# The bank shared by a graph network's second product and its last block of sums: zeroed each group, or overwritten and its sums carried away

## The chip, the core and the metric

The kernel runs on one core of a Trainium2 chip. The metric is the time of one execution on the device in microseconds (us), the median of several runs. TensorE multiplies matrices into PSUM (8 banks of 512 f32 columns by 128 partitions); VectorE, ScalarE and GpSimd work element by element, and the latter also issues the indirect transfers (gathers); SyncE (SP) and ScalarE issue plain ones.

## The reference, cut to what matters

Four graph layers in a row work on 3125 nodes with 16 features and 103125 edges sorted by one end. The second, called L1, is the one that the change touches. It has four layers itself, with 128 hidden features:

```python
h = h @ emb_w + emb_b
for i in range(4):
    ef = concat([h[row], h[col], edge_attr])
    ef = silu(ef @ edge_w1[i] + edge_b1[i])
    ef = silu(ef @ edge_w2[i] + edge_b2[i]) * edge_mask
    agg = segment_sum(ef, row, num_segments=n)
    nf = silu(concat([h, agg]) @ node_w1[i] + node_b1[i])
    h = (h + nf @ node_w2[i] + node_b2[i]) * node_mask
```

## The kernel before

Nodes are padded to 25 blocks of 128 (NB = 25, NP = 3200); the last block has 53 real nodes (3125 - 3072). Edges are in tiles of 128, and three tiles (M3) make a group: 280 groups (G3) in each of the four layers, in turns of U3 = 8, 35 turns (K3). Turns 0, 1 and 34 are written out; the others are a hardware loop, so each engine has a branch after every eight groups.

update(layer) writes two tables to memory: p_tab and q_tab, h times the two halves of the first edge weight. edge_mlp(layer) then does for each group, with one semaphore per kind of work:

- SP and ScalarE load the p_tab blocks (pb) for the group; SP loads also q_tab blocks (qb), and rows for the one-hot matrices. GpSimd gathers rows of q_tab by index (L1613), two tiles of a group, and three in every fourth group (nine gathers in four groups). VectorE writes the indices (L1764) five groups ahead.
- VectorE builds the one-hot matrices ohn and oht (L1784, L1785) one group ahead, and ohm (L1793, three per group).
- TensorE's first(): all parts of the first product are added into z1, 384 columns of bank 7 (L1655, L1658, L1660, and the gathers by a transposing matmul, L1663). It waits for the gathers ahead of L1663, and raises m_z1.
- ScalarE's one(): silu from z1 into h1 (L1729), raises m_h1.
- TensorE's second(): three matmuls of h1 with w2 into z2 (L1673), raises m_z2.
- VectorE's add(): z2 + b2 into h2 (L1771), raises m_add; then it waits for that add, and sets z2 to zero (L1774), raising m_zero.
- ScalarE's two(): silu of h2 in place (L1734), raises m_h2.
- TensorE's sums(): three matmuls of h2 with ohm (L1683), each added onto the columns of the block that the tile's edges belong to; the address is a register. It raises m_sum.

PSUM is full: the sums of all 25 blocks fill columns 0 to 3199 for the whole of a layer, z1 is columns 3584 to 3967 and z2 3200 to 3583. So bank 6 (columns 3072 to 3583) holds both the last block's sums and z2. Matmuls with start=False add onto what stands there; a start=True in that bank would touch the bookkeeping of the whole bank. That is why z2 is set to zero by VectorE and the second product is added onto the zeros.

The order on each queue, for group n, is:

- TensorE: first(n), sums(n-3), second(n-1). sums(n-3) waits for zero(n-2), second(n-1) for the same.
- VectorE: add(n-2) with its memset, build(n+1), indices(n+5), build_m(n-2).
- ScalarE: two(n-2), one(n), and issues of loads between.

After the groups, update(layer) copies the sums out of PSUM (bank 6 by VectorE, L1960) and goes on with the node part. Each line below carries the number that the profile uses.

Of the kernel before, what the change touches and what calls it, by code (L numbers as in the profile page):

```python
# [54 lines left out]
def gnn_kernel(nc, a, out):  # L55

    with ExitStack() as ctx:
# [1441 lines left out]
        with ExitStack() as st:  # L1499
# [63 lines left out]
        m_idx, m_oht, m_ohm, m_z1, m_h1, m_z2, m_add, m_zero, m_h2, m_sum = (  # L1563
            sem("m_" + n) for n in ("idx", "oht", "ohm", "z1", "h1", "z2", "add", "zero", "h2", "sum"))
        m_got = [sem(f"m_got{h}") for h in range(U3)]
        m_pl, m_sp, m_act = ([sem(f"m_{n}{q}") for q in range(U3 // 2)] for n in ("pl", "sp", "act"))
        Z1, Z2 = 3584, NP

        def edge_mlp(layer, we36, w2, b1, b2):
# [18 lines left out]
            with ExitStack() as st:  # L1588
# [11 lines left out]
                z1, z2 = ps[:, Z1:Z1 + GW], ps[:, Z2:Z2 + GW]  # L1600

                with nc.Block() as block:
# [38 lines left out]
                    def _(pe):  # L1641
# [23 lines left out]

                        def second(k, h):

                            n = k * U3 + h
                            if layer or here(k, h, 1):
                                pe.wait_ge(m_zero, g0 + n)  # L1670
                            pe.wait_ge(m_h1, g0 + n + 1)
                            for j in range(M3):
                                m = pe.matmul(z2[:, j * P:(j + 1) * P], h1[:, h % 2, j * P:(j + 1) * P], w2, start=False, stop=True, skip_group_check=True)  # L1673
                            m.then_inc(m_z2, 1)

                        def sums(k, h, after=2):
# [3 lines left out]
                            pe.wait_ge(m_zero, g0 + n + after)  # L1680
# [10 lines left out]
                        def step(k, h):  # L1691
                            if h % 2 == 0 and here(k, h, 2):
                                take(*moved(k, h, -2))
                            first(k, h)
                            if here(k, h, 3):
                                sums(*moved(k, h, -3))
                            if here(k, h, 1):
                                second(*moved(k, h, -1))
                        turns(pe, step, K3, U3)
                        take(K3 - 1, U3 - 2)  # L1700
                        sums(K3 - 1, U3 - 3)
                        second(K3 - 1, U3 - 1)
                        sums(K3 - 1, U3 - 2)
                        take(K3 - 1, U3 - 1)
                        sums(K3 - 1, U3 - 1, 1)
# [51 lines left out]
                    def _(dve):  # L1757
# [8 lines left out]
                        def add(k, h):  # L1766
                            n = k * U3 + h
                            if here(k, h, 2):
                                dve.wait_ge(m_sum, g0 + n - 1)
                            dve.wait_ge(m_z2, g0 + n + 1)  # L1770
                            dve.tensor_tensor(h2[:, h % 2, :, :], z2.rearrange("p (j f) -> p j f", j=M3),  # L1771
                                              b2[:, None, :].to_broadcast([P, M3, HID]), ALU.add).then_inc(m_add, 1)
                            dve.wait_ge(m_add, g0 + n + 1)
                            dve.memset(z2, 0.0).then_inc(m_zero, 1)  # L1774
# [29 lines left out]

                        for h in range(5):
                            indices(0, h)
# [5 lines left out]
                        build_m(K3 - 1, U3 - 1)  # L1812

        with ExitStack() as st:
# [14 lines left out]
            b2 = sb("b2", [P, L, HID], F32, st)  # L1829
            xT = sb("xT1", [FIN, NP], F32, st)  # L1830
# [347 lines left out]
```

## Time and profile before

| | us |
|---|---|
| median of 3 runs | 8277.64 |
| lowest and highest | 8270.27, 8279.68 |
| the profiled execution | 8273.71 |
| its span | 8272.0 |
| TensorE busy, whole span | 6199.3 |
| TensorE weight loads busy | 5285.4 |
| GpSimd busy | 5228.1 |
| VectorE busy | 5187.0 |
| ScalarE busy | 2895.5 |

The span is the time from the first to the last instruction in the profile; the execution's own time has 1.7 us around it. Busy times are sums over the whole span, in which four functions of very different character follow each other, so their shares have to be read by stretch. In a row of grouped instructions, out<-in are the program's names, x is the count, then come the busy us, the mean ns of one, and the idle us of that engine just before them with what ended that idle time; "issue" means that nothing that the profile shows ended it. One matmul of f32 operands counts as two records.

### The profile page before, as it was taken

Reading aid. Unit: us, or ns where it says so; the run is one execution under the profiler, and the core shown is the slowest. Engines: PE = TensorE matmul, PEld = TensorE weight load, DVE = VectorE, ACT = ScalarE, POOL = GpSimd, SP = SyncE. Lnnn points to the kernel's source line nnn. Section 1 sums busy time; section 2 is a strip of 40 time slices with the busy share of each in tenths; the row PEclk is TensorE's granted clock in tenths of the full one; section 3 lists DMA queues with packets and bytes.
Section 4 is the critical chain, followed back from the end, with each engine's and each line's share of the span. In section 5 each row is a group of like instructions: output and inputs, shape, how many; then the busy total and the mean of one; then the engine's idle time right before and its main releaser. Section 6 shows DMA issues by size and latency. Waiting matters only on the chain. (4 is left out here: it accounts for less than half of the span.)

```text
span 8272.0 us, 234007 instructions
## 1 busy us (share of the span) xinstructions
PE 6199.3 (75%) x55084; PEld 5285.4 (64%) x55143; DVE 5187.0 (63%) x14678; ACT 2895.5 (35%) x8539; POOL 5228.1 (63%) x7407
## 2 busy tenths in 40 slices
PE   2222215767789998999899989999976667888998
PEld 1111113555478886888688868887575556887998
DVE  6333346867567775777577757776432225998998
ACT  3222202545433333333333333333233332222554
POOL 3777754756477776777677767776677774222554
PEclk7555556555599999999999999999555556999999
DMA  5000013434378786878688768886300001332332
GB/s 162 5 3 3 3 38 107 120 96 120 88 221 220 220 220 176 222 222 222 179 222 222 222 174 227 222 222 183 101 6 7 7 7 38 82 82 56 73 72 59
DMA packets 1322718, 1020.15 MB, mean 123 GB/s; under 512 B 479756, under 2 KB 1223586, under 8 KB 1321696
## 3 DMA queue, kind: packets, MB, share of 16 engines
q1 hardware_dynamic: 938010, 667.14, 29.2%
q0 software_dynamic: 134272, 178.98, 9.2%
q10 hardware_dynamic: 250308, 172.51, 7.2%
q8 instruction: 57, 0.93, 0.0%
q14 instruction: 71, 0.58, 0.0%
HBM read 951.88 MB, written 73.77 MB: 124 GB/s over the span
## 5 line engine op out<-in xcount | busy, mean ns | idle before, releaser
L1613 POOL DMA_INDIRECT qg<-q_tab,qidx x2520 | 2421.6, 961 | 873.1 <-issue 610.1
L1163 PE MATMUL ps<-rhs_i,ohi 128*128 128x128 f32 (+2 forms) x8640 | 1215.2, 266 | 209.8 <-issue 197.7
L1734 ACT ACTIVATE h<-h 128x384 f32<-128x384 f32 x1120 | 585.8, 523 | 1910.4 <-DVE h L1771 1824.0
L1163 PEld LDWEIGHTS ps<-rhs_i,ohi 128*128 128x128 f32 (+1 forms) x8640 | 998.6, 162 | 342.2 <-issue 281.2
L1683 PE MATMUL ps<-ohm,h 128*128 128x128 f32 x6720 | 1029.8, 289 | 226.0 <-issue 213.2
L1129 POOL COPY near<-x 128x48 bf16 x2160 | 676.0, 351 | 774.3 <-PE ps L1152 432.2
L1771 DVE TENSOR_TENSOR h<-ps,b 128x384 f32<-128x384 f32 x1120 | 623.9, 557 | 823.2 <-PE ps L1673 779.0
L1683 PEld LDWEIGHTS ps<-ohm,h 128*128 128x128 f32 x6720 | 834.5, 191 | 456.5 <-issue 456.3
L1314 POOL DMA_INDIRECT got_m<-y_tab,idx_m x832 | 831.1, 999 | 330.3 <-issue 248.7
L407 POOL DMA_INDIRECT list_by_src<-ring,rpos x808 | 783.1, 969 | 333.2 <-issue 253.9
L1793 DVE TENSOR_SCALAR ohm<-iota_row,loc_p,w_p 128x128 f32<-128x128 f32 x3360 | 966.0, 350 | 0.1
L1673 PE MATMUL ps<-w,h 128*128 128x128 f32 x6720 | 936.5, 276 | 0.0
L1224 DVE TENSOR_TENSOR ohi<-iota_row,dst_i 128x512 f32<-128x512 f32 (+1 forms) x1080 | 927.9, 859 | 0.0
L1338 PE MATMUL ps<-rhs_m,ohi_m 128*128 x2880 | 662.0, 403 | 321.3 <-ACT rhs_m L1370 290.4
L1338 PEld LDWEIGHTS ps<-rhs_m,ohi_m 128*128 128x128 f32 x2880 | 634.6, 328 | 350.2 <-issue 350.1
L1673 PEld LDWEIGHTS ps<-w,h 128*128 128x128 f32 x6720 | 843.3, 193 | 0.5 <-DVE ps L1774 0.2
L1658 PE MATMUL ps<-oht,pb 128*128 128x128 bf16 x10080 | 750.1, 220 | 0.0
L1729 ACT ACTIVATE h<-ps,b 128x384 f32<-128x384 f32 x1120 | 649.9, 580 | 209.0 <-PE ps L1663 116.1
L1658 PEld LDWEIGHTS ps<-oht,pb 128*128 128x128 bf16 x10080 | 661.1, 98 | 82.6 <-issue 1.9
L1400 DVE TENSOR_TENSOR ohi_m<-iota_row,dst_i 128x512 f32<-128x512 f32 x360 | 249.1, 693 | 727.4 <-PE ps L1338 727.4
L1219 DVE TENSOR_SCALAR oht_i<-places_i,iota_p 128x512 bf16<-128x512 bf16 (+1 forms) x1080 | 510.4, 473 | 192.9 <-PE ps L1163 161.4
L1127 POOL COPY near<-z 128x384 bf16 x720 | 345.4, 509 | 365.4 <-PE ps L1152 303.5
(448 smaller groups left out, 8921.1 us busy)
## 6 DMA issues: line engine op xcount, KB each, us to landing
pb<-p_tab ACTq DMA_DIRECT2D x1680, 96.0 KB
pb<-p_tab SPq DMA_DIRECT2D x1680, 96.0 KB
places<-place_by_turn SPq DMA_DIRECT2D x560, 192.0 KB
places_i<-place_by_meeting SPq DMA_DIRECT2D x360, 256.0 KB, 3.4
places_i<-place_by_meeting SPq DMA_DIRECT2D x720, 128.0 KB, 3.1
qb<-q_tab SPq DMA_DIRECT2D x840, 64.0 KB
qg<-q_tab,qidx POOLq DMA_INDIRECT x2520
nears<-near_by_turn SPq DMA_DIRECT2D x560, 64.0 KB
```

Of the source, the lines that this page charges most:

```text
L407: pool.indirect_dma_start(list_s[:, :], IndirectOffsetOnAxis(ap=rpos[:, h, c:c + 1], axis=0), ring[:, h, c, :], None).then_inc(scattered[h ...
L1129: m = pool.tensor_copy(near[:, h, j, :], table[:, bass.ds(at[j], 48)])
L1163: m = pe.matmul(ps[:, bass.ds(to[j], width)], ohi[:, h, j, :], rhs[:, h, j, 0:width], start=False, stop=True, skip_group_check=True)
L1224: dve.tensor_tensor(ohi[:, h, :, :], iota_row[:, None, :].to_broadcast([P, M, P]), dst_i[:, bass.ds(n * M, M)][:, :, None].to_broadcast([P ...
L1314: pool.indirect_dma_start(got[:, h, j, :], None, y_tab, IndirectOffsetOnAxis(ap=idx[:, h, j:j + 1], axis=0)).then_inc(d_got[h], 16)
L1338: m = pe.matmul(ps[:, bass.ds(to[j], 32)], ohi[:, h, j, :], rhs[:, bass.ds(at[j], 1), :].rearrange("p t f -> p (t f)"), start=False, stop= ...
L1613: pool.indirect_dma_start(qg[:, h, j, :], None, q_tab, IndirectOffsetOnAxis(ap=qidx[:, h, j:j + 1], axis=0)).then_inc(m_got[h], 16)
L1658: pe.matmul(z1[:, j * P:(j + 1) * P], pb[:, h, j, q_ * HID:(q_ + 1) * HID], oht[:, h, j * P:(j + 1) * P], start=False, stop=False)
L1673: m = pe.matmul(z2[:, j * P:(j + 1) * P], h1[:, h % 2, j * P:(j + 1) * P], w2, start=False, stop=True, skip_group_check=True)
L1683: m = pe.matmul(ps[:, bass.ds(to[M3 * (1 - h % 2) + j], P)], h2[:, h % 2, j, :], ohm[:, h % 2, j, :], start=False, stop=True, skip_group_c ...
L1729: act.activation(h1[:, h % 2, :], z1, ACT.Silu, bias=b1).then_inc(m_h1, 1)
L1793: m = dve.tensor_scalar(ohm[:, h % 2, j, :], iota_row[:, :], loc_p[:, bass.ds(t, 1)], w_p[:, bass.ds(t, 1)], ALU.is_equal, ALU.mult)
```

## The change

- The second product is written with start=True, so z2 needn't be zero: the memset and m_zero go.
- After the three matmuls of second(), fresh() writes zeros with start=True to `part`, the 53 real columns of the last block's sums in bank 6 (a bf16 matmul of a zero tile). m_z2 is raised by it. The sums that follow add onto these zeros.
- So what the last block has gathered must leave the bank each group: add() has a second tensor_tensor, `rim += part`, with rim a tile [128, 53] in SBUF, and it is that one that raises m_add.
- TensorE's order becomes first(n), second(n-1), sums(n-3). second(n-1) waits for m_add of group n-2. The sums wait for ohm and h2 alone.
- add(n-2) waits for m_sum of group n-4, and by the order on TensorE that covers m_z2 of n-2.
- rim is zeroed at the start of a layer, and at its end VectorE adds the last part; update() copies rim in place of bank 6's columns. The columns of aggT behind N are zeroed once.

```diff
--- before.py
+++ after.py
@@ -1560,13 +1560,13 @@
                         root_step(act, b_to + 2)
 
 
-        m_idx, m_oht, m_ohm, m_z1, m_h1, m_z2, m_add, m_zero, m_h2, m_sum = (
-            sem("m_" + n) for n in ("idx", "oht", "ohm", "z1", "h1", "z2", "add", "zero", "h2", "sum"))
+        m_idx, m_oht, m_ohm, m_z1, m_h1, m_z2, m_add, m_h2, m_sum = (
+            sem("m_" + n) for n in ("idx", "oht", "ohm", "z1", "h1", "z2", "add", "h2", "sum"))
         m_got = [sem(f"m_got{h}") for h in range(U3)]
         m_pl, m_sp, m_act = ([sem(f"m_{n}{q}") for q in range(U3 // 2)] for n in ("pl", "sp", "act"))
-        Z1, Z2 = 3584, NP
-
-        def edge_mlp(layer, we36, w2, b1, b2):
+        Z1, Z2, FEW = 3584, NP, N - (NB - 1) * P
+
+        def edge_mlp(layer, we36, w2, b1, b2, rim):
 
 
             g0, k0 = layer * G3, layer * K3
@@ -1598,6 +1598,7 @@
                 h1 = sb(f"h1{layer}", [P, 2, GW], F32, st)
                 h2 = sb(f"h2{layer}", [P, 2, M3, HID], F32, st)
                 z1, z2 = ps[:, Z1:Z1 + GW], ps[:, Z2:Z2 + GW]
+                part = ps[:, NP - P:NP - P + FEW]
 
                 with nc.Block() as block:
                     @block.gpsimd
@@ -1663,21 +1664,24 @@
                                 m = pe.matmul(z1[:, j * P:(j + 1) * P], qg[:, h, j, :], ident[:, :], start=False, stop=(j == gathered(h) - 1), is_transpose=True)
                             m.then_inc(m_z1, 1)
 
+                        def fresh():
+
+                            return pe.matmul(part, nothing[:, 0:P], nothing[:, 0:FEW], start=True, stop=True)
+
                         def second(k, h):
 
                             n = k * U3 + h
                             if layer or here(k, h, 1):
-                                pe.wait_ge(m_zero, g0 + n)
+                                pe.wait_ge(m_add, g0 + n)
                             pe.wait_ge(m_h1, g0 + n + 1)
                             for j in range(M3):
-                                m = pe.matmul(z2[:, j * P:(j + 1) * P], h1[:, h % 2, j * P:(j + 1) * P], w2, start=False, stop=True, skip_group_check=True)
-                            m.then_inc(m_z2, 1)
-
-                        def sums(k, h, after=2):
+                                pe.matmul(z2[:, j * P:(j + 1) * P], h1[:, h % 2, j * P:(j + 1) * P], w2, start=True, stop=True)
+                            fresh().then_inc(m_z2, 1)
+
+                        def sums(k, h):
 
                             n = k * U3 + h
                             pe.wait_ge(m_ohm, g0 + n + 1)
-                            pe.wait_ge(m_zero, g0 + n + after)
                             pe.wait_ge(m_h2, g0 + n + 1)
                             for j in range(M3):
                                 m = pe.matmul(ps[:, bass.ds(to[M3 * (1 - h % 2) + j], P)], h2[:, h % 2, j, :], ohm[:, h % 2, j, :],
@@ -1692,17 +1696,19 @@
                             if h % 2 == 0 and here(k, h, 2):
                                 take(*moved(k, h, -2))
                             first(k, h)
+                            if here(k, h, 1):
+                                second(*moved(k, h, -1))
                             if here(k, h, 3):
                                 sums(*moved(k, h, -3))
-                            if here(k, h, 1):
-                                second(*moved(k, h, -1))
                         turns(pe, step, K3, U3)
                         take(K3 - 1, U3 - 2)
+                        second(K3 - 1, U3 - 1)
                         sums(K3 - 1, U3 - 3)
-                        second(K3 - 1, U3 - 1)
+                        pe.wait_ge(m_add, g0 + G3)
+                        fresh()
                         sums(K3 - 1, U3 - 2)
                         take(K3 - 1, U3 - 1)
-                        sums(K3 - 1, U3 - 1, 1)
+                        sums(K3 - 1, U3 - 1)
 
                     @block.scalar
                     def _(act):
@@ -1767,11 +1773,13 @@
                             n = k * U3 + h
                             if here(k, h, 2):
                                 dve.wait_ge(m_sum, g0 + n - 1)
-                            dve.wait_ge(m_z2, g0 + n + 1)
+                            else:
+                                dve.wait_ge(m_z2, g0 + n + 1)
                             dve.tensor_tensor(h2[:, h % 2, :, :], z2.rearrange("p (j f) -> p j f", j=M3),
-                                              b2[:, None, :].to_broadcast([P, M3, HID]), ALU.add).then_inc(m_add, 1)
-                            dve.wait_ge(m_add, g0 + n + 1)
-                            dve.memset(z2, 0.0).then_inc(m_zero, 1)
+                                              b2[:, None, :].to_broadcast([P, M3, HID]), ALU.add)
+                            if layer or here(k, h, 1):
+                                dve.wait_ge(m_add, g0 + n)
+                            dve.tensor_tensor(rim, rim, part, ALU.add).then_inc(m_add, 1)
 
                         def build(k, h):
                             n, q = k * U3 + h, h // 2
@@ -1802,6 +1810,7 @@
                             if here(k, h, 2):
                                 build_m(*moved(k, h, -2))
 
+                        v_chain(dve, dve.memset(rim, 0.0))
                         for h in range(5):
                             indices(0, h)
                         build(0, 0)
@@ -1810,6 +1819,8 @@
                         build_m(K3 - 1, U3 - 2)
                         add(K3 - 1, U3 - 1)
                         build_m(K3 - 1, U3 - 1)
+                        dve.wait_ge(m_sum, g0 + G3)
+                        v_chain(dve, dve.tensor_tensor(rim, rim, part, ALU.add))
 
         with ExitStack() as st:
             hT = sb("hidT", [P, NP], F32, st)
@@ -1827,6 +1838,7 @@
             third = sb("third", [36, 3], BF16, st)
             part36 = sb("part36", [36, 2], F32, st)
             b2 = sb("b2", [P, L, HID], F32, st)
+            rim = sb("rim", [P, N - (NB - 1) * P], F32, st)
             xT = sb("xT1", [FIN, NP], F32, st)
             pq_out = [sem(f"pq_out{i}") for i in range(4)]
             pq_n = [0] * 4
@@ -1835,6 +1847,7 @@
                 @block.vector
                 def _(dve):
                     v_chain(dve, dve.memset(maskT[:, N:NP], 0.0))
+                    v_chain(dve, dve.memset(aggT[:, N:NP], 0.0))
                     v_chain(dve, dve.memset(eat[:, :, :], 0.0))
                     v_chain(dve, dve.memset(we36[:, :], 0.0))
                     for q, (lo, hi) in enumerate(((0, 12), (12, 24), (24, 36))):
@@ -1956,8 +1969,8 @@
                     def _(dve):
                         if not first:
                             for i in (0, 2, 4, 6):
-                                n = min(512, NP - 512 * i)
-                                dve.tensor_copy(aggT[:, 512 * i:512 * i + n], banks[i][:, 0:n]).then_inc(u_sum_v.sem, 1)
+                                n = min(512, N - 512 * i)
+                                dve.tensor_copy(aggT[:, 512 * i:512 * i + n], rim[:, :] if i == 6 else banks[i][:, 0:n]).then_inc(u_sum_v.sem, 1)
 
                         if first:
                             dve.wait_ge(mask_in, 32)
@@ -2018,7 +2031,7 @@
 
             update(-1)
             for layer in range(L):
-                edge_mlp(layer, we36[:, layer * HID:(layer + 1) * HID], w2[:, layer, :], b1[:, layer:layer + 1], b2[:, layer, :])
+                edge_mlp(layer, we36[:, layer * HID:(layer + 1) * HID], w2[:, layer, :], b1[:, layer:layer + 1], b2[:, layer, :], rim[:, :])
                 update(layer)
             nodes([(hT, wout[:, :])], FIN, 0)
             b_to, b_fr = to_act.base(1), from_act.base(1)
```

## Rows read from the trace of the kernel before

**Rows 1.** The page's costliest groups: busy us, mean ns, then idle us before and releasers.

```profile
L1613 POOL DMA_INDIRECT qg<-q_tab,qidx x2520 | 2421.6, 961 | 873.1 <-issue 610.1
...
L1314 POOL DMA_INDIRECT got_m<-y_tab,idx_m x832 | 831.1, 999 | 330.3 <-issue 248.7
```

**Rows 2.** Busy time by stretch, one of L1's four steady ones: us, engines, clock, DMA.

```profile
3185.00:4010.00 825.00, 758.79 (x7186) 674.37 (x7186) 575.07 (x2154) 308.22 (x559) 601.59 (x625) 1.00 0.79 219
```

**Rows 3.** Groups of instructions by line, 3200 to 3900 us, same columns.

```profile
L1683 PE MATMUL ps<-ohm,h 128*128 128x128 f32 x1434 | 219.6, 289 | 44.1 <-issue 41.2
```

**Rows 4.** Timeline of one group: start us, us, engine, line.

```profile
3272.35 0.56 DVE L1771 TENSOR_TENSOR h<-ps,b 128x384 f32<-128x384 f32 x1 [0.70 <-PE ps L1673]
...
3272.94 0.52 ACT L1734 ACTIVATE h<-h 128x384 f32<-128x384 f32 x1 [1.75 <-DVE h L1771]
...
3273.06 0.38 DVE L1774 MEMSET ps<- 128x384 f32 x1 [0.15 <-DVE h L1771]
...
3273.09 0.38 PE L1663 MATMUL ps<-ident,qg 128*128 128x128 f32 x2
3273.35 0.22 DVE L1784 TENSOR_SCALAR ohn<-nears,iota_p 128x128 f32<-128x128 bf16 x1
3273.47 0.26 DVE L1785 TENSOR_SCALAR oht<-places,iota_p 128x384 bf16<-128x384 bf16 x1
3273.53 0.58 ACT L1729 ACTIVATE h<-ps,b 128x384 f32<-128x384 f32 x1
...
3273.64 0.93 PE L1683 MATMUL ps<-ohm,h 128*128 128x128 f32 x6 [0.17 <-issue]
...
3274.41 0.83 PE L1673 MATMUL ps<-w,h 128*128 128x128 f32 x6
...
3275.07 0.33 PE L1655 MATMUL ps<-eat,we 128*128 128x384 bf16 x1
...
3275.28 0.56 DVE L1771 TENSOR_TENSOR h<-ps,b 128x384 f32<-128x384 f32 x1 [0.68 <-PE ps L1673]
```

**Rows 5.** Timeline of TensorE where the loop branch falls.

```profile
3280.26 0.83 PE L1673 MATMUL ps<-w,h 128*128 128x128 f32 x6
3281.43 0.33 PE L1655 MATMUL ps<-eat,we 128*128 128x384 bf16 x1 [0.33 <-issue]
3281.60 0.67 PE L1658 MATMUL ps<-oht,pb 128*128 128x128 bf16 x9
3282.10 0.44 PE L1660 MATMUL ps<-ohn,qb 128*128 128x128 f32 x2
...
3283.93 0.33 PE L1655 MATMUL ps<-eat,we 128*128 128x384 bf16 x1
```

**Rows 6.** Timeline of GpSimd, the gathers.

```profile
3289.40 0.94 POOL L1613 DMA_INDIRECT qg<-q_tab,qidx  x1 [0.80 <-DVE qidx L1764]
...
3324.41 0.94 POOL L1613 DMA_INDIRECT qg<-q_tab,qidx  x1 [1.71 <-DVE qidx L1764]
...
5757.05 0.94 POOL L1613 DMA_INDIRECT qg<-q_tab,qidx  x1 [0.30 <-issue]
```

**Rows 7.** Groups of instructions by line, whole span.

```profile
L1976 DVE TENSOR_TENSOR left<-ps,p_out 128x128 f32<-128x128 f32 x100 | 28.3, 289 | 72.9 <-ACT q_out L1946 72.4
```

**Rows 8.** Waits of SP's queue, 3200 to 3900 us: us, times, longest.

```profile
SPq L1626 <- PE ps L1663: 97.3, 111, 1.5
```

**Rows 9.** Timeline of TensorE, last sums of the fourth layer.

```profile
5775.29 0.93 PE L1683 MATMUL ps<-ohm,h 128*128 128x128 f32 x6 [0.18 <-issue]
```

**Rows 10.** Timeline of the second layer's beginning.

```profile
3178.94 0.97 POOL L1613 DMA_INDIRECT qg<-q_tab,qidx  x1 [3.50 <-DVE qidx L1764]
...
3186.51 0.50 PE L1655 MATMUL ps<-eat,we 128*128 128x384 bf16 x1 [5.41 <-DMA pb<-p_tab]
```

**Rows 11.** Timeline of the third function, GpSimd and ScalarE.

```profile
6302.05 0.94 POOL L1314 DMA_INDIRECT got_m<-y_tab,idx_m  x1 [0.30 <-issue]
...
6304.56 0.85 ACT L1365 ACTIVATE gate_m<-got_m,hea_s 128x1 f32<-128x1 f32 x4 [3.15 <-DMA got_m<-y_tab,idx_m]
```

## The prediction

> **What bounds the kernel now.** I read the page's costliest groups first [rows 1]: GpSimd's gathers (L1613) lead them. The second layer function, L1, runs from about 2288 to 5776 us, four layers of 280 groups (1120 calls of each line), and there no engine is full. So I cut it into the four steady stretches [rows 2]: in each of 825 us TensorE is busy 759, GpSimd 602, VectorE 575, ScalarE 308, at a granted clock of 1.00 and a DMA share of 0.79. TensorE at 92% has about 66 us of holes per layer. The grouped rows of 700 us [rows 3] say where: 44 us ahead of the sums' matmuls (L1683), under "issue", that is, on a semaphore that the profile does not name.
>
> The timeline of one group names it [rows 4]. The add (L1771) starts at 3272.35, the memset of the second product's columns ends at 3273.06 + 0.38 = 3273.44, and the sums start at 3273.64. The transposed gathers (L1663) had begun at 3273.09; a run of such matmuls gives way to the next about 0.16 before its recorded end (L1673 lasts 0.83, L1655 begins 0.66 later), so the sums could have begun at 3273.31. TensorE waits 0.33 us for m_zero. The loop that sets the pace is: add 0.56, own semaphore 0.15, memset 0.38, to TensorE 0.20, sums 0.77, second product 0.66, and 0.21 from the next group's first matmul (3275.07) to the next add (3275.28). That is 2.93, and 2.92 to 2.93 is the spacing of L1655. What TensorE needs by itself is seen where the loop branch has put it late, so that the memset is no longer waited for [rows 5]: 3281.43 to 3283.93, 2.50 us. The branch itself costs TensorE 1.17 - 0.67 = 0.50 us in eight groups (3280.26 to 3281.43).
>
> Behind TensorE stands GpSimd, and close. Its gathers of 0.94 follow each other with holes of 0.30 us [rows 6], and the holes are 0.30 too where VectorE's indices are called the releaser. So 0.30 is GpSimd's own. Over all of L1 there are 2520 gathers of 0.961 us with 873.1 us of holes [rows 1]. Two kinds of longer hole exist. One of 0.80 (3289.40) stands once or so in a turn of eight groups and ahead of a group's first gather: that is a wait for the indices, which VectorE writes five groups ahead. The other is 1.7 to 1.95 us long and stands ahead of the second gather of a group, where the code waits for nothing; it comes every 99 gathers, at the same places in every layer, 6 times per layer (the one at 3324.41 in rows 6). I take it as GpSimd's own.
>
> **GpSimd's floor.** 4 x 630 gathers x (0.961 + 0.305) = 3190.3 us, and 24 holes x about 1.54 above 0.305 = 37.0, together 3227 us; per group 3227 / 1120 = 2.88. What it takes now is 2421.6 + 873.1 less the four holes ahead of a layer's first gather (about 3.5 each, 14.1; one in rows 10) = 3280.6. The difference, 54 us, is all that its waits for TensorE's pace are worth.
>
> **The change, part by part.** *The memset goes* (1120 x 0.378) and with it VectorE's wait for its own add (0.15). *The add into rim comes*: tensor_tensor of 128x53 f32 from PSUM. The trace has 128x384 at 0.56 us (L1771) and 128x128 at 0.289 (L1976) [rows 4, 7], a slope of 1.06 ns a column, so 53 columns are about 0.21 us. At most it is L1976's 0.29; how little it is doesn't matter, since TensorE's own time, below, is then the longer. It waits only for the rim add before it, long done, and VectorE's instructions without a wait between them overlap a little (L1784 of 0.22 at 3273.35, L1785 at 3273.47 [rows 4]), so I let it end 0.69 after the add starts; if it can't overlap, 0.77. *fresh()* is one bf16 matmul of 53 columns and its weight load: nine L1658 take 0.50 us (3281.60 to 3282.10) [rows 5], so 0.06; nothing at the least, since a weight load can go ahead; at worst weight load 0.10 and matmul 0.33, unhidden like a lone L1655, 0.42. *The order* first, second, sums moves the wait of VectorE's add from m_z2 to m_sum, but both are the end of TensorE's step; and the wait for VectorE moves from the sums to the second product, at the same place behind first(). The sums lose their m_zero wait and wait for ohm and h2 of three groups back, both done a step earlier.
>
> The new loop: 0.69, to TensorE 0.20, second 0.66, fresh 0.06, sums 0.77, 0.21 = 2.59. TensorE's own: 2.50 + 0.06 + 0.50/8 = 2.62. So TensorE and VectorE want 2.62 to 2.67 per group where GpSimd wants 2.88: **GpSimd becomes the bound**, and the change is worth what it lets GpSimd give.
>
> The Trainium skill, "VectorE: DVE Perf Modes", section "The DRAIN you can't avoid", says that the next VectorE operation does not start until the pipe is empty. By that the rim add ends at 0.77, the loop is 2.67 and the sum below stays; here L1785 starts 0.10 before L1784 ends, so the trace does not quite agree.
>
> What else is queued: m_add now comes from the rim add, so ScalarE's second silu (L1734) starts about 0.13 later than now (3272.94), ends 1.24 after the add, and L1729, which now starts 1.18 after it (3273.53), slips by 0.06; its result is wanted by the next L1655 at 2.4. Covered by sums and second product; without that cover it would cost its 0.06. VectorE's queue behind the adds (ohn, oht, indices, ohm) moves earlier by about 0.4. SP's queue waits for TensorE 97.3 us in 700 (111 times) [rows 8], so it has room for 2.88.
>
> **Edges of a layer, x4.** Now GpSimd is done well ahead: last gather ends 5757.05 + 0.94 = 5757.99, sums end 5775.29 + 0.93 = 5776.22, 18.2 later [rows 6, 9]. Bound by GpSimd, that lead is used up (it begins as 3186.51 - 3178.94 = 7.6 us [rows 10], and 0.2 per group eats it within some 40 groups). After the last gather: landing 1.6 (in the third function ScalarE starts 1.57 after a gather's end [rows 11]; bounds 0.3 and 2.8), transposes 0.34, second 0.72, sums 0.77 = 3.43; 0.21 + 0.69 + 0.20 + 0.72 + 0.77 = 2.59 for group 279's second product and the sums of 277; 0.21 + 0.69 + 0.20 + 0.06 + 0.77 + 0.93 for the rest = 2.86: 8.9, and the last rim add with its semaphores 0.36: 9.2. Gain 9.0. The memset of rim ahead of the indices delays the first gather by about 0.25 (a small operation and 0.15). Net 8.7 per layer, 35 in all. The other edits (aggT's pad once, 53 columns instead of 128 in one copy) are under 0.5 us.
>
> **Sum.** 54 + 35 = 89 us. The profiled execution took 8273.7 (span 8272.0 and 1.7 around it), so 8185; against the median of 8277.6, **8188 us**.
>
> **Rivals.** A change of 0.2% (16.6 us) is about what a measurement can tell from none.
> 1. *GpSimd binds* (8188, own range 8165 to 8215, from the landing, 0.30 or 0.31 for a hole, and the 24 long holes): 0.68.
> 2. *The VectorE-TensorE loop still binds.* With every price at its upper end, 0.56 + 0.15 + 0.29 + 0.20 + 0.66 + 0.15 + 0.77 + 0.21 = 2.99, nothing is won; from 2.88 up it decides. For it: every group now waits there. Against: a wait and 0.17 of length are plainly gone. At 2.90 for the present mean of 2.935 (825 us, less edges, for 280 groups) it gives 39 us, and no lead is used: 8238. 0.10.
> 3. *Gathers grow.* They are the bound, and L1314's take 999 ns where these take 961 [rows 1]. 38 ns x 2520 = 96 us eats the 89: 8285, no change. Against: until a layer's first long hole, 87 gathers run free in 3289.4 - 0.5 - 3178.94 = 110.0 us [rows 6, 10], 1.264 each, the same price. 0.08.
> 4. *Gathers shrink.* Most take 0.94 [rows 6] and the mean is 0.961, so at most 21 ns x 2520 = 53 us: 8135. 0.08. The Trainium skill, "DMA: Bandwidth & Descriptors", section "SWDGE vs HWDGE vs iDMA", says that GpSimd writes its descriptor rings in SBUF and that VectorE can lock it out in its two-port modes. By that rule a denser VectorE would lengthen gathers and a removed memset would shorten them; no row here separates the two.
> 5. *Slower: fresh() is not pipelined.* A bf16 weight load and matmul wedged between f32 runs, on TensorE, each group, at 0.42 us: 2.56 + 0.42 = 2.98 against 2.935, x 1120 = +50 us: 8328. It decides from 0.375 us. For it: such a pair stands alone nowhere in the trace. Against: L1655 follows f32 matmuls 0.66 behind, as they follow each other. 0.06.
>
> **Numbers.** Faster: 0.68 + 0.08 + 0.07 of rival 2 = 0.83. Same: rival 3 and a little of 2, 0.09. Slower: 0.08, rival 5 and the upper tails of 2 and 3. The range of 8140 to 8265 takes in 1, nearly all of 4 and the faster part of 2, and leaves out some 0.19.
>
> **What the profile of the changed kernel would show.** GpSimd's holes ahead of L1613 all 0.30 but for the 24 long ones, "DVE qidx" as releaser nearly gone; TensorE waiting for gathers ahead of the transposes in first(), and no wait ahead of sums or second product; spacing of groups 2.88 with two-gather groups shorter and three-gather groups longer; last gather to last sums about 9 us; rim adds of 0.21. I am wrong if the wait reappears ahead of the second product (rival 2), if L1613's mean moves from 961, or if the pair of fresh() takes over 0.3 us.

## The result, and the profile after

Before, in the runs beside it: 8274.6 us (8270.3 to 8279.7, four runs). After: **8127.3 us** (8124.0 to 8131.0, four runs). The ratio is 0.9822, with a 95% interval of 0.9805 to 0.9839: 147 us, 1.8%. The forecast was 8188 with a range of 8140 to 8265. It had the direction and the new bound, and a gain of 89 us where 147 came; the time lies below the range. One later execution, of the changed kernel with TensorE's old order, took 10256 us at a mean granted clock of 0.54, where the others had 0.79; it is left out below and not explained.

The profiled execution took 8131.0 (span 8129.3, against 8272.0: 142.7 less). The page's costliest groups (busy, mean ns of one, idle before and its releasers) show GpSimd's gathers, the sums' matmuls and the transposes:

```profile
L1614 POOL DMA_INDIRECT qg<-q_tab,qidx x2520 | 2398.8, 952 | 781.9 <-issue 647.9
...
L1687 PE MATMUL ps<-ohm,h 128*128 128x128 f32 x6720 | 1024.6, 289 | 0.7 <-issue 0.7
...
L1664 PE MATMUL ps<-ident,qg 128*128 128x128 f32 x2520 | 479.6, 281 | 158.4 <-DMA qg<-q_tab,qidx 154.9
```

The wait ahead of the sums (L1687) is gone: 0.7 us in all of L1, where it was 44.1 in 700 us alone [rows 3]. TensorE now waits for gathered rows ahead of the transposes. GpSimd's idle time fell by 91.2 and its busy time by 22.8 [rows 1]. A layer fits in less than 825 us, so the busy time of each engine is read over 780 us of the second layer (columns as in [rows 2]):

```profile
3150.00:3930.00 780.00, 735.53 (x7428) 691.77 (x7428) 535.84 (x2147) 306.68 (x557) 589.05 (x619) 1.00 0.83 229
```

GpSimd is busy 589 and idle 191 there, at 1.26 us a gather, and TensorE is still at 94%. The groups by line of 3200 to 3900 us:

```profile
L1614 POOL DMA_INDIRECT qg<-q_tab,qidx x557 | 529.9, 951 | 169.9 <-issue 146.1 <-DVE qidx L1770 22.6 <-PE ps L1664 1.2
...
L1782 DVE TENSOR_TENSOR rim<-rim,ps 128x53 f32<-128x53 f32 x248 | 49.7, 200 | 0.0
L1669 PE MATMUL ps<-nothing 128*128 128x53 bf16 x248 | 46.6, 188 | 0.0
```

169.9 us of idle time ahead of 557 gathers is 0.305 each, whoever is called the releaser, so that is the floor. The longest single waits of GpSimd in that stretch, by the waits view, are 0.3 too:

```profile
POOL qg L1614 <- issue: 146.1, 479, 0.3
POOL qg L1614 <- DVE qidx L1770: 22.6, 74, 0.3
```

Where the kernel before has one of its long holes, behind the 113th gather of the layer (1.71 us [rows 6]), the timeline of GpSimd has nothing; the last line is the same gather:

```profile
3275.84 0.94 POOL L1614 DMA_INDIRECT qg<-q_tab,qidx  x1 [0.30 <-issue]
3277.08 0.94 POOL L1614 DMA_INDIRECT qg<-q_tab,qidx  x1 [0.30 <-issue]
3278.33 0.99 POOL L1614 DMA_INDIRECT qg<-q_tab,qidx  x1 [0.30 <-issue]
```

The timeline of TensorE (start, length, then any wait) has two groups without a wait, 2.61 apart, and one of three gathers that waits:

```profile
3324.82 0.33 PE L1656 MATMUL ps<-eat,we 128*128 128x384 bf16 x1
...
3325.98 0.83 PE L1678 MATMUL ps<-w,h 128*128 128x128 f32 x6
3326.65 0.19 PE L1669 MATMUL ps<-nothing 128*128 128x53 bf16 x1
3326.68 0.91 PE L1687 MATMUL ps<-ohm,h 128*128 128x128 f32 x6
3327.43 0.33 PE L1656 MATMUL ps<-eat,we 128*128 128x384 bf16 x1
...
3330.04 0.33 PE L1656 MATMUL ps<-eat,we 128*128 128x384 bf16 x1
3330.20 0.67 PE L1659 MATMUL ps<-oht,pb 128*128 128x128 bf16 x9
3331.29 0.55 PE L1664 MATMUL ps<-ident,qg 128*128 128x128 f32 x3 [0.42 <-DMA qg<-q_tab,qidx]
...
3333.12 0.33 PE L1656 MATMUL ps<-eat,we 128*128 128x384 bf16 x1
```

VectorE's two adds and ScalarE's two silu of the first of these groups, from the timeline of all engines:

```profile
3325.02 0.56 DVE L1778 TENSOR_TENSOR h<-ps,b 128x384 f32<-128x384 f32 x1 [0.81 <-PE ps L1687]
3325.49 0.20 DVE L1782 TENSOR_TENSOR rim<-rim,ps 128x53 f32<-128x53 f32 x1
3325.73 0.52 ACT L1740 ACTIVATE h<-h 128x384 f32<-128x384 f32 x1 [1.58 <-DVE rim L1782]
...
3326.32 0.58 ACT L1735 ACTIVATE h<-ps,b 128x384 f32<-128x384 f32 x1
```

TensorE's timeline at the end of the fourth layer, behind the last gather (5620.92 + 0.94 = 5621.86):

```profile
5623.42 0.55 PE L1664 MATMUL ps<-ident,qg 128*128 128x128 f32 x3 [0.38 <-DMA qg<-q_tab,qidx]
...
5626.18 0.94 PE L1678 MATMUL ps<-w,h 128*128 128x128 f32 x6 [0.77 <-DVE rim L1782]
...
5629.95 0.96 PE L1687 MATMUL ps<-ohm,h 128*128 128x128 f32 x6 [0.17 <-issue]
5632.45 1.12 PE L1908 MATMUL ps<-hidT,wn 128*128 128x512 f32 x2 [1.54 <-DVE aggT L1973]
```

**Where the 142.7 us came from.** From the first gather's start to the last one's end the four layers took 825.7, 818.1, 818.7 and 818.2 us before, and 791.2, 791.3, 791.5 and 791.8 after: 114.7 less. Each gather's own hole, sorted by its length in the two timelines, splits it. Short holes above the floor of 0.305 gave 54.6 (there are none after). The 24 long ones gave 37.0 (none after). The gathers themselves gave 22.8. These make 114.4 of it. Of the 142.7, the other 28.0 lie outside the gathers, at the layers' edges.

### The profile page after: what moved, and what is told of

Same layout as the page of the kernel before. It is cut to its first block and busy times, and to the rows that moved or that the text cites. A ratio compares the mean times of both kernels' runs of the same rounds, so it can differ in the third digit from the quotient of the medians.

```text
span 8129.3 us, 235796 instructions
## 1 busy us (share of the span) xinstructions
PE 6145.4 (76%) x56208; PEld 5382.7 (66%) x56267; DVE 5038.0 (62%) x14687; ACT 2897.6 (36%) x8539; POOL 5208.7 (64%) x7407
## 5 line engine op out<-in xcount | busy, mean ns | idle before, releaser
L1687 PE MATMUL ps<-ohm,h 128*128 128x128 f32 x6720 | 1024.6, 289 | 0.7 <-issue 0.7
L407 POOL DMA_INDIRECT list_by_src<-ring,rpos x808 | 784.2, 971 | 333.0 <-issue 254.2
L1687 PEld LDWEIGHTS ps<-ohm,h 128*128 128x128 f32 x6720 | 839.0, 192 | 14.7 <-issue 1.4
L1664 PE MATMUL ps<-ident,qg 128*128 128x128 f32 x2520 | 479.6, 281 | 158.4 <-DMA qg<-q_tab,qidx 154.9
```

What stands on the lines that cost most here:

```text
L407: pool.indirect_dma_start(list_s[:, :], IndirectOffsetOnAxis(ap=rpos[:, h, c:c + 1], axis=0), ring[:, h, c, :], None).then_inc(scattered[h ...
L1687: m = pe.matmul(ps[:, bass.ds(to[M3 * (1 - h % 2) + j], P)], h2[:, h % 2, j, :], ohm[:, h % 2, j, :], start=False, stop=True, skip_group_c ...
```

## The experiments

What each is for: the 37.0 us of long holes were forecast to stay, so they are the question. Either VectorE's memset, which the change removes, brought them out, or they come when GpSimd is held back, by whatever. The other questions are the price of fresh(), the order, and what lengthened the gathers.

The chips were not alike. On chips 13 and 1 the kernel before takes 8274 and 8279 us; on chips 14, 6 and 10 it takes 10259, 10393 and 10411. Each time and ratio below is against the kernel before on the same chip.

**The memset put back** (chip 13), behind the add of the changed kernel, with its semaphore:

```diff
-                    b2[:, None, :].to_broadcast([P, M3, HID]), ALU.add)
+                    b2[:, None, :].to_broadcast([P, M3, HID]), ALU.add).then_inc(m_zero, 1)
+                            dve.wait_ge(m_zero, g0 + n + 1)
+                            dve.memset(z2, 0.0)
```

> The changed kernel with the memset of z2 put back between VectorE's add and the rim add, with the wait for the add's own semaphore ahead of it; nothing is left out of the result. My theory: the loop of VectorE and TensorE is again longer than GpSimd's time. From the group spacing of 2.61 that the changed kernel shows when nothing waits for a gather, plus 0.15 + 0.38 = 3.14 us against 2.83 now: 8127 + 0.31 x 1120 + about 30 for the edges = 8500 us (8440 to 8540). Rival, that the memset was hidden all along and the gain came from the order: under 8200. On the 24 holes of 1.7 to 1.95 us ahead of second gathers: they should be back by both explanations that I hold open, that the memset causes them and that holding GpSimd back causes them; if they stay away, both are wrong.

Measured: 8363.5 us, ratio 1.0108 (1.0091 to 1.0125). That is 1.1% slower than before, but 137 us less than the 8500 expected, and outside the expected range. VectorE's timeline:

```profile
3403.92 0.56 DVE L1778 TENSOR_TENSOR h<-ps,b 128x384 f32<-128x384 f32 x1 [0.58 <-PE ps L1687]
3404.63 0.38 DVE L1781 MEMSET ps<- 128x384 f32 x1 [0.15 <-DVE h L1778]
3404.92 0.20 DVE L1784 TENSOR_TENSOR rim<-rim,ps 128x53 f32<-128x53 f32 x1
...
3406.92 0.56 DVE L1778 TENSOR_TENSOR h<-ps,b 128x384 f32<-128x384 f32 x1 [0.59 <-PE ps L1687]
```

The loop is 3.00, not 3.14. The rim add starts 0.09 before the memset's recorded end, and the next second product of TensorE (3405.17) follows the rim add's end at 0.05, where [rows 4] had led me to 0.20. The loop binds again, and the long holes are back: 6 per layer, 39.5 us in all, at gathers of a mean of 948 ns. So this run says that a bound loop brings the holes, but not whether the memset does.

**fresh() six times** (chip 13):

```diff
+                            for _ in range(5):
+                                fresh()
                             fresh().then_inc(m_z2, 1)
```

> The changed kernel with fresh() issued six times in place of once; nothing is left out of the result. This slows TensorE by 5 x 0.06 = 0.28 to 0.30 us a group and puts no memset anywhere: about 2.90 + 0.06 for the branch = 2.96 us a group, so that GpSimd is held back again: 8127 + 0.13 x 1120 + up to 30 for the edges = 8290 us (8230 to 8320). If the long holes come from GpSimd being held back, 24 of them are there again and gathers have a mean near 0.961. If they come from VectorE's memset, there are none, and the mean is near 0.950. If a fresh() costs far more than 0.06 the time shows it: at 0.19 each, the recorded length, 8127 + 0.78 x 1120 + 30 = 9030 us.

Measured: 8130.9, ratio 0.9825 (0.9809 to 0.9842), the time of the changed kernel. TensorE's timeline shows why:

```profile
3400.51 0.32 PE L1669 MATMUL ps<-nothing 128*128 128x53 bf16 x6
3400.66 0.91 PE L1689 MATMUL ps<-ohm,h 128*128 128x128 f32 x6
```

Six take 0.15 us from start to the sums' start, 0.026 each. TensorE wants 2.74 per group then (2.80 with the branch), still under 2.83, and nothing is held back: no hole over 0.32 in any layer. TensorE is busy 762.7 of the 780 us where the changed kernel has 735.5, and the layers take 789 to 791: 27 us more of TensorE's busy time cost nothing. My expectation had gone by the prediction's price of 0.06 for each, more than twice what was measured.

**The order of before** (chip 13): first product, sums, second product, the rest as in the changed kernel, with fresh() now ahead of the sums.

```diff
-                            fresh().then_inc(m_z2, 1)
+                            m.then_inc(m_z2, 1)
...
+                            if clear:
+                                pe.wait_ge(m_add, g0 + n + 2)
+                                fresh()
...
-                            if here(k, h, 1):
-                                second(*moved(k, h, -1))
                             if here(k, h, 3):
                                 sums(*moved(k, h, -3))
+                            if here(k, h, 1):
+                                second(*moved(k, h, -1))
```

> The changed kernel with TensorE's old order first, sums, second: fresh() stands ahead of the sums, which wait for the rim add, and VectorE's add waits for m_z2 again; nothing is left out of the result. Theory: the wait for VectorE stands behind first() either way, the loop stays at about 2.6 us and GpSimd binds at 2.83, so the time is 8127 within 16, with the holes of GpSimd all at 0.30. Rival, that the order carries part of the gain: waits ahead of the sums and 8160 or more.

Measured: 8122.9, 8123.0 and 8131.1, ratio 0.9823 (0.9804 to 0.9843). The layers take 790 to 792, without a hole over 0.32. The order is worth nothing here. Since the run with the memset put back lost the whole gain, what matters is that the memset and its wait left the loop.

**On chip 14**, four kernels: twelve fresh() (11 more in place of the 5 above), a memset that no one waits for, and both kernels with two gathers in every group.

```diff
+                            dve.memset(aside, 0.0)
```

stands between the add and the rim add, on columns of a tile in SBUF that is idle there (a tile of its own behind the rim add, off the loop, has no room left in SBUF, so that form was not measured), and

```diff
-                return 3 if h % 4 == 3 else 2
+                return 2
```

leaves out the third gather of every fourth group, so that those blocks' rows are not what the reference wants.

> The changed kernel with fresh() issued twelve times; nothing is left out of the result. Six of them left the time alone and took 0.155 us together, 0.026 each, so twelve add about 0.29 us a group: TensorE needs 2.61 + 0.29 + 0.06 for the branch = 2.96 against GpSimd's 2.83, and GpSimd is held back with no memset anywhere. Time: 8127 + 0.13 x 1120 + 15 to 30 for the edges = 8295 us (8250 to 8320). If the long holes ahead of second gathers come from holding GpSimd back, there are 24 again; if they come from VectorE's memset, there are none.

> The changed kernel with one more memset of 128x384 f32 per group on VectorE, into columns of a tile in SBUF that nothing uses meanwhile, between its two adds; nothing is left out of the result. VectorE's side of the loop has 0.24 us or more to spare against TensorE's 2.61 and more against GpSimd's 2.83, so GpSimd should still bind. If a memset disturbs GpSimd by itself (gathers that start just behind it take up to 1.19 in the kernel before), the gathers' mean rises from 0.951 to 0.960 or more and the time to 8150 to 8200 us, and long holes return if they are its work. If it was only the place of the memset in the loop that cost time: mean 0.95, no long hole, 8127 within 8.

> The changed kernel with two gathers in every group; it leaves out the third gather of every fourth group, and so a part of the first product of that tile. GpSimd then needs 2 x 1.257 = 2.51 us a group, less than TensorE's 2.60 on average (three groups of 2.61, one of 2.34, and 0.06 for the branch), so this shows what the loop alone costs after the change: 8127 - 0.22 x 1120 = 7880 us (7850 to 7930), and no wait ahead of the transposes. If something else than GpSimd stands behind the 2.83 (loads, ScalarE), less is won than 100 us.

> The kernel before with two gathers in every group; it leaves out the same part. There the loop over memset and semaphores sets the pace at 2.93, so GpSimd's shorter time should change nothing: 8274 within 12. With e7 it gives the change's worth where GpSimd doesn't bind, about 390 us or 0.33 a group. Long holes: if they come with GpSimd being held back they are there, at other places; if they belong to places in the order of gathers, every 99th still.

Measured, against 10258.8: 10642.3, ratio 1.0391 (1.0358 to 1.0423); 10349.1, 1.0101 (1.0072 to 1.0130); 9924.3, 0.9684 (0.9657 to 0.9712); 9797.6, 0.9556 (0.9524 to 0.9587). All four miss what was expected of them, and none tests what it was made for: L1 moves 140 to 164 GB/s there, against 219 in [rows 2]. Between the two kernels with two gathers the changed one is the slower by 1.3% (9924.3 against 9797.6). The first three come again on chip 1, and the last one on chips 6 and 10, below.

**Twelve fresh() again** (chip 1): no memset anywhere, but TensorE's step longer than GpSimd's floor. It is the run that tells the two theories of the long holes apart.

> The changed kernel with fresh() issued twelve times, again, since the last measurement was on a chip whose transfers are slower (the kernel before took 10259 us there). Same expectation: TensorE needs about 2.61 + 0.29 + 0.06 = 2.96 us a group against GpSimd's 2.83, GpSimd is held back with no memset anywhere, 8295 us (8250 to 8320). If the long holes ahead of second gathers come from holding GpSimd back, there are 24 again; if from VectorE's memset, none.

Measured: 8252.5, ratio 0.9970 (0.9957 to 0.9982), just at the lower edge of the expected range. GpSimd's timeline:

```profile
3559.42 0.94 POOL L1614 DMA_INDIRECT qg<-q_tab,qidx  x1 [0.30 <-issue]
3560.67 0.94 POOL L1614 DMA_INDIRECT qg<-q_tab,qidx  x1 [0.30 <-issue]
3563.55 0.94 POOL L1614 DMA_INDIRECT qg<-q_tab,qidx  x1 [1.94 <-PE ps L1664]
```

Six long holes in every layer again, 9.3 to 9.8 us of excess a layer, and 14 to 19 us of short ones. No memset runs in L1's groups. So the holes need no memset. Against six fresh() only TensorE's own time is longer, and the 24 holes are the difference: in L1 they come with a GpSimd that is held back.

**The memset aside again** (chip 1):

> The changed kernel with one more memset of 128x384 f32 per group into an idle SBUF tile between VectorE's two adds, again, on a chip with transfers as in the first measurements. If a memset disturbs GpSimd by itself: mean gather 0.960 or more and 8150 to 8200 us, with long holes if they are its work. If it was only its place in the loop that cost time: mean 0.95, no long hole, 8127 within 8.

Measured: 8197.2, ratio 0.9905 (0.9888 to 0.9921). VectorE's timeline shows that the memset did not stay aside:

```profile
3561.62 0.56 DVE L1778 TENSOR_TENSOR h<-ps,b 128x384 f32<-128x384 f32 x1 [0.35 <-PE ps L1687]
3562.21 0.38 DVE L1782 MEMSET nT<- 128x384 f32 x1
3562.50 0.15 DVE L1783 TENSOR_TENSOR rim<-rim,ps 128x53 f32<-128x53 f32 x1
...
3564.46 0.56 DVE L1778 TENSOR_TENSOR h<-ps,b 128x384 f32<-128x384 f32 x1 [0.54 <-issue]
```

The rim add starts 0.88 after the add, where it started 0.47 after it, and the loop is 2.84. I had reckoned 0.24 us of slack, and it was used up. The loop again just holds GpSimd: 21 long holes, layers of 802 to 804, gathers of 952 ns as after. A memset in every group did not lengthen the gathers. In the first layer GpSimd runs with holes under 0.33 up to its 204th gather, and the place behind the 113th passes without a hole; the five behind it have theirs. The third layer fits less well: its hole behind the 113th is 1.92, with nothing over 0.33 ahead of it.

**Two gathers in every group** of the changed kernel (chip 1), so that GpSimd's floor drops to 2 x 1.26 = 2.5 us per group:

> The changed kernel with two gathers in every group (it leaves out the third gather of every fourth group), again. GpSimd needs 2.51 us a group, TensorE about 2.60: 7880 us (7850 to 7930) and no wait ahead of the transposes. If something else than GpSimd stands behind the 2.83, less than 100 us is won.

Measured: 7933.6, ratio 0.9584 (0.9568 to 0.9600), just above the expected range. The window of 600 us in the second layer:

```profile
3200.00:3800.00 600.00, 590.92 (x6029) 559.41 (x6029) 437.62 (x1760) 250.84 (x454) 433.45 (x455) 1.00 0.88 242
```

TensorE is busy 98%, and the 600 us hold 228 groups, 2.63 each. The third gather thus costs the changed kernel 202 us. Here too GpSimd is held back, and here too there are long holes: five in every layer, behind the 113th gather and every 100th from there, and one of 1.32 behind the 60th in the second layer. They keep nearly to the count of gathers, though one group in four has a gather fewer.

**The changed kernel again** (chip 1):

> The changed kernel itself beside the other three, as it is. 8127 within 8 where the kernel before takes 8274. If this chip has the slower transfers (the kernel before at 10200 or more), the loads bind in both and the change is worth little or nothing: 10259 within 100, since TensorE then waits for loads in either order.

Measured: 8135.4, ratio 0.9826 (0.9810 to 0.9843), layers of 792 to 793, no hole over 0.32; that is 0.4 us over the expected 8127 within 8, where the kernel before takes 4 us more too. The gain and the absence of holes repeat on a second chip.

**Before with two gathers** (chips 6 and 10), and the changed kernel beside it on chip 10, to learn what the change does to the loop alone:

> The kernel before with two gathers in every group (it leaves out the third gather of every fourth group), again, on a chip with transfers as in the first measurements. The loop over the memset sets the pace at 2.93, so GpSimd's shorter time changes nothing: 8278 within 12. With e11 (7934) it gives the change's worth where GpSimd doesn't bind: about 345 us, against 147 where it does. Rival: if the 2.93 were partly GpSimd's, 8200 or less.

> The kernel before with two gathers in every group (it leaves out the third gather of every fourth group), once more. On a chip where the kernel before takes 8274 to 8279: 8278 within 12, since the loop over the memset sets the pace; with e11 (7934) the change is worth about 345 us where GpSimd doesn't bind. Rival: 8200 or less, if the 2.93 were partly GpSimd's. On a chip with slow transfers: about 9800 to 9920, as measured twice.

> The changed kernel itself. Where the kernel before takes 8274 to 8279: 8130 within 8. On a chip with slow transfers (the kernel before above 10200): TensorE waits for loads in both, and in the variants with two gathers the new one was the slower there (9924 against 9798), so between 10250 and 10450, no gain or a loss of up to 1.5%.

Measured: 9922.1 against 10393.3, ratio 0.9543 (0.9505 to 0.9582); 9941.9 against 10411.1, 0.9554 (0.9538 to 0.9570), both just above the 9920 expected at most for such a chip; and the changed kernel 10519.4, **1.0099** (1.0080 to 1.0118), which is slower than before and outside what was expected (10250 to 10450). Both chips were again of the slower kind, so the loop alone was not measured at full transfer speed. The changed kernel's window of 700 us on chip 10, the groups on its page, and TensorE's longest wait in the window by the waits view:

```profile
3900.00:4600.00 700.00, 499.13 (x4170) 462.44 (x4171) 295.67 (x1209) 172.93 (x313) 329.97 (x350) 0.86 0.53 145
```

```profile
L1614 POOL DMA_INDIRECT qg<-q_tab,qidx x2520 | 2388.0, 948 | 2586.9 <-DVE qidx L1770 1805.8
...
L1735 ACT ACTIVATE h<-ps,b 128x384 f32<-128x384 f32 x1120 | 650.9, 581 | 1952.9 <-remote 1481.0
```

```profile
PEld ps L1656 <- issue: 205.5, 62, 5.3
```

No engine is at its bound there. 145 GB/s are moved at a DMA share of 0.53, and the gathers are as short as ever with more idle time before them than they last. TensorE waits 205.5 us of the 700 ahead of first(), which waits for the loads, for oht and for ScalarE's first silu. That fits loads that come late, but no view names them. The granted clock is 0.86 on average there, so a part of the stretch is at the lower of its two levels, against 1.00 (2.4 GHz) in the window of the changed kernel above, and the sums' matmuls take 316 ns in place of 289, so a part of the longer time is TensorE's. Why the change then loses 1% is not settled; neither the old order nor a kernel without the rim add was run on such a chip.

## Why the prediction was wrong, by its own steps

**GpSimd becomes the bound: right.** Every hole is 0.30, TensorE waits for gathers ahead of the transposes, sums and second product wait for nothing. TensorE's own step without the branch, 2.56 forecast, measured 2.61. The forecast waits of 54 us measured 54.6. The rim add took 0.20 (0.21), and fresh() 0.03 (0.06, rival 5: 0.42). ScalarE's second silu ends 1.23 after the add (1.24 forecast), but its first one starts 1.30 after it, a slip of 0.12 from 1.18 where 0.06 was forecast; TensorE's next step (3327.43) waits for nothing, so it is covered, as forecast.

**The step that failed: "I take it as GpSimd's own"**, said of the long holes. With it 37.0 us were put into the floor and the sum, as a fixed part. The changed kernel has none of them in L1. Twelve fresh() brought them back with no memset, and six, which do not hold GpSimd back, did not. So in L1 the 37.0 us were a price of being held back.

The trace of before could not have settled it, but it could have shown that the term was open. In L1 the only free run of gathers, the first 87, was too short to reach the 113th. Two other functions of that same kernel have longer free runs of indirect transfers, and they say opposite things. In the third, GpSimd gathers 832 times with nothing to hold it back. Its waits from 5840 to 6918 us:

```profile
POOL got_m L1314 <- issue: 247.5, 812, 0.3
POOL got_m L1314 <- ACT idx_m L1358: 4.0, 13, 0.3
POOL got_m L1314 <- ACT rhs_m L1370: 0.6, 2, 0.3
```

827 holes, 0.305 each, and none longer than 0.3, where one in 99 would have made eight. The 330.3 us of idle time in [rows 1] are 77.1 ahead of the first gather and 253.2 at 0.305. But in the first function GpSimd issues 808 indirect writes (L407) with nothing over 0.31 between them, and yet has seven long holes, behind the 113th and every 112th from there, in the kernel after as well. From its timeline in the kernel before, and its waits from 141 to 1180 us:

```profile
284.84 0.96 POOL L407 DMA_INDIRECT list_by_src<-ring,rpos  x1 [0.30 <-issue]
287.47 0.98 POOL L407 DMA_INDIRECT list_by_src<-ring,rpos  x1 [1.66 <-issue]
```

```profile
POOL list_by_src L407 <- issue: 253.9, 802, 1.7
```

So "only when held back" is shown for L1's gathers and is no rule for GpSimd. By the third function's row the 37.0 us would have been counted as given back, and the forecast had been 8151; by the first one's they stay, 8188. The prediction looked at neither, and gave the term no chance and no part of the range.

**Gathers: assumed to stay at 961 ns, 952 measured.** This is rival 4, of which 22.8 of its 53 us came, at the same time as rival 1. I had listed the two as exclusive, and that is the other reason why the range was too short: 8188 less 37 less 23 is 8128. What the Trainium skill ("DMA: Bandwidth & Descriptors", section "SWDGE vs HWDGE vs iDMA") says of VectorE and GpSimd's descriptors was my reason for rival 4. The runs clear the memset by itself: 952 with one in SBUF in each group, 948 with the memset in PSUM, 948 with twelve fresh() and no memset. They do not clear VectorE. Of the 265 gathers of 1.0 us or more in the kernel before, 264 run while VectorE builds ohm (L1793), as 1616 of all 2520 do; the 904 that don't overlap it take 944 ns on average. In the changed kernel it is 134 of 136. One such gather in the kernel before, of 1.15 us, from the timeline:

```profile
3214.15 0.38 DVE L1774 MEMSET ps<- 128x384 f32 x1 [0.16 <-DVE h L1771]
3214.26 1.15 POOL L1613 DMA_INDIRECT qg<-q_tab,qidx  x1 [0.30 <-issue]
...
3214.81 0.85 DVE L1793 TENSOR_SCALAR ohm<-iota_row,loc_p,w_p 128x128 f32<-128x128 f32 x3
```

So the long gathers go with that work of VectorE, and there are fewer of them after the change. That it is the cause is not shown: no run takes the building of ohm away, and most gathers that overlap it are not longer.

**Edges: 35 forecast, 28 measured.** The last gather to the last sums' end took 5630.91 - 5621.86 = 9.05 us (8.9 forecast, and the landing 1.56 for 1.6). But from there to the next part it is 1.54 where it was 1.07, which is rim's part added last and then aggT. And from the first gather of the first layer on, this execution began 2.3 us later than before's. The gaps between a layer's last gather and the next one's first fell by 10.6, 7.2 and 5.9, and the one behind the fourth layer by 6.6.

So the sum goes: 89 + 0.6 (short holes) + 37.0 + 22.8 - 7.0 = 142.4, of 142.7 in the profiled executions. The rest to 147 is these executions against their medians (8273.7 for 8274.6, and 8131.0 for 8127.3).

**Rivals 2, 3 and 5** are out: no wait in the loop, gathers shorter instead of longer, fresh() nearly free. Rival 2 became true in the run with the memset aside, 2.84 at 8197. TensorE's own step had room for the 0.13 of five more fresh() and not for the 0.29 of eleven more, so the margin was about 0.2 us per group.

**Open.** What the long hole is (mostly 1.4 to 1.7 us above 0.30, nearly at a fixed count of transfers; in L1 with GpSimd held back, in the first function without). Why some gathers beside the building of ohm are longer. What the change is worth where GpSimd does not bind, at full transfer speed. Why it costs 1% on chips with slower transfers.

## What to carry to other kernels

Before a periodic hole is put into an engine's floor, look through the whole program for every stretch in which that engine runs free for longer than the period. If there is none, or if they disagree, as the first and third functions do here, the hole's sum is an uncertain term and belongs in the range. When the bound moves from one loop to an engine behind it, the gain is all that the engine loses by being held back, and that may be more than the waits that are named. Rivals that act on different terms add, and a range made of them one at a time is too narrow. Time a change on more than one chip: here it is 1.8% faster in the first comparison, 1.7% on chip 1, and 1.0% slower on chip 10, where the kernel before itself takes 10.41 ms.

## What the runs showed of the hardware

- Indirect gathers go back to back at 0.95 + 0.305 us for 630 of them in a row, in the four kernels where GpSimd binds. In the five on the faster chips where L1 holds GpSimd back, a hole of mostly 1.7 to 2.0 us comes behind the 113th and every 99th (or 100th) from there. The first function's 808 indirect writes have such a hole of 1.66 to 1.68 behind every 112th although nothing holds them back, and the third function's 832 gathers have none.
- 264 of the 265 gathers of 1.0 us or more in the kernel before run beside VectorE's f32 tensor_scalar of 128x128 (L1793); gathers without it take 944 ns.
- A bf16 matmul of 53 columns with its weight load, recorded at 0.19 us, costs 0.025 to 0.03 us between f32 runs: six took 0.15 us and twelve 0.30 (in the run on chip 1). The recorded length of this short matmul is not what it costs in the stream.
- Three of the five chips ran the kernel before at 10.26 to 10.41 ms in place of 8.27, in all seven executions on each, with L1 moving 140 to 164 GB/s (in the variants measured there) against 219.
